# Both halves of a row of exponentials in a row on VectorE, and its sum scaled on ScalarE

## What is computed

```python
x = L0_attn_x                                    # (4, 2048, 256) fp32
x = x + _layernorm(_L0_attn_ref(_layernorm(x)))  # first stage
x = x + _layernorm(_L0_ffn_ref(_layernorm(x), ...))

def _L0_attn_ref(x):
    scores = jnp.einsum('bid,bjd->bij', x, x)
    attn = jax.nn.softmax(scores, axis=1)
    context = jnp.einsum('bij,bjd->bid', attn, x)
    return context
```

## Time and profile before

| | |
|---|---|
| median of 3 runs | 3178.43 us (3177.80 to 3181.57) |
| profiled execution, span | 3177.2 us |
| PE busy | 2982.5 us (94%) |
| DVE busy | 2656.8 us (84%) |
| ACT busy | 1847.9 us (58%) |
| POOL busy | 1754.4 us (55%) |
| TensorE's mean granted clock | 0.976 of full speed |
| first stage, until its last store is issued | 707.65 us |
| exponential stage of each of four batches | 70.2 us |

### The profile page before, as it was taken

One profiled execution on the slowest core, in us unless ns is written; L12 is line 12 of the kernel. 1 busy time (PEld: TensorE's weight loads), 2 busy tenths in 40 slices (PEclk: granted clock), 3 DMA queues, 4 the chain that ended last, 5 costly groups with the idle time before them and its releaser, 6 DMA issues.

```text
span 3177.2 us, 79721 instructions
## 1 busy us (share of the span) xinstructions
PE 2982.5 (94%) x24952; PEld 2581.8 (81%) x24952; DVE 2656.8 (84%) x7754; ACT 1847.9 (58%) x4226; POOL 1754.4 (55%) x2083
## 2 busy tenths in 40 slices
PE   6898989783899999999999999999999999999997
PEld 3676767573688888888888888888888888888886
DVE  6878788755788888888888888899998999999895
ACT  4233241402566666666666666666676676676673
POOL 1231314024566666666666666676676676676773
PEclk9999999995899999999999999999999999999999
DMA  1120202025111111111111111222112212122221
GB/s 38 38 70 28 80 14 87 4 83 205 33 50 49 53 51 49 52 48 49 54 50 50 50 48 50 56 56 60 56 55 57 65 55 60 55 55 60 63 56 46
DMA packets 273326, 177.65 MB, mean 56 GB/s; under 512 B 95758, under 2 KB 271090, under 8 KB 272754
## 3 DMA queue, kind: packets, MB, share of 16 engines
q1 hardware_dynamic: 273138, 175.50, 19.0%
HBM read 104.08 MB, written 54.54 MB: 50 GB/s over the span
## 4 chain that ended last, share of the span: by engine, by line
PE 72%; POOL 1%; issue 1%; DVE 0%; DMA 0%; ACT 0%; POOLq 0%; SPq 0%; DVEq 0%; ACTq 0%
PE b_ps L824 17%; PE b_ps L899 14%; PE b_ps L910 10%; PE b_ps L852 8%; PE b_ps L840 7%; PE b_ps L878 6%; PE b_ps L865 6%; PE b_ps L809 2%; PE b_ps L802 2%; PE b_ps L791 1%; POOL b_sq L1145 0%; POOL b_rn L1178 0%; POOL b_t L1167 0%; POOL b_kr L1183 0%; DVE b_probs L1093 0%
## 5 line engine op out<-in xcount | busy, mean ns | idle before, releaser
L957 ACT ACTIVATE b_probs<-b_probs,b_negmax 128x256 f32<-128x256 f32 x1024 | 506.0, 496 | 78.3 <-DVE b_negmax L1093 77.5
L824 PE MATMUL b_ps<-b_wqkv,b_hT_hi 128*128 128x512 f32 x1536 | 493.0, 402 | 1.0 <-DVE b_hT_lo L981 1.0
L899 PE MATMUL b_ps<-b_h2T,b_w 128*128 128x256 f16 x4224 | 473.0, 273 | 6.5 <-DMA b_h2T<-b_xh_hl 6.4
L899 PEld LDWEIGHTS b_ps<-b_h2T,b_w 128*128 128x128 f16 x4224 | 413.6, 98 | 55.1 <-DMA b_h2T<-b_xh_hl 6.8
L1145 POOL TENSOR_TENSOR b_sq<-b_sq 128x512 f32<-128x512 f32 (+5 forms) x768 | 419.3, 546 | 62.4 <-ACT b_sq L938 22.3
L1178 POOL TENSOR_TENSOR b_rn<-b_ss_min,b_mhalf 128x16 f32<-128x16 f32 x128 | 377.2, 2947 | 108.9 <-DVE b_ss_min L1005 108.7
L1106 DVE TENSOR_SCALAR b_probs<-b_probs,b_rinv 128x256 f32<-128x256 f32 x1024 | 409.6, 442 | 18.2
L1155 POOL TENSOR_TENSOR b_rstd<-b_var,b_mhalf 128x1 f32<-128x1 f32 x128 | 72.2, 564 | 552.3 <-DVE b_var L1066 552.3
L407 PE MATMUL a_ps<-a_xn_hl,a_E 128*128 128x256 f16 x3072 | 352.5, 277 | 18.9 <-DVE a_E L290 18.9
L407 PEld LDWEIGHTS a_ps<-a_xn_hl,a_E 128*128 128x128 f16 x3072 | 303.3, 99 | 58.5 <-issue 19.9
L910 PE MATMUL b_ps<-b_w,b_hid 128*128 128x256 f32 x1536 | 342.2, 379 | 1.2 <-DVE b_hid L1129 1.2
(11 more groups left out here) (137 smaller groups left out, 6191.6 us busy)
## 6 DMA issues: line engine op xcount, KB each, us to landing
b_hx<-xs_dram SPq DMA_DIRECT2D x256, 64.0 KB, 1.9
b_rot<-rot_dram SPq DMA_DIRECT2D x128, 128.0 KB, 2.1
b_xr<-xs_dram SPq DMA_DIRECT2D x128, 128.0 KB, 2.1
xp_dram<-b_xp SPq DMA_DIRECT2D x128, 128.0 KB, 1.7
b_h<-xp_dram SPq DMA_DIRECT2D x256, 64.0 KB, 1.8
a_x_res<-in_L_attn_x_dram SPq DMA_DIRECT2D x64, 128.0 KB, 2.2
x_dram<-a_x SPq DMA_DIRECT2D x64, 128.0 KB, 1.7
xs_dram<-a_xo SPq DMA_DIRECT2D x64, 128.0 KB, 1.8
```

The costliest lines, as they stand in the source:

```text
L824: last = nc.tensor.matmul(ps[:, bank, :], hT[:, k, :], wqkv[:, ds(layer(s), 1), part, k, bank * INNER:(bank + 1) * INNER], start=(k == 0 a ...
L899: last = nc.tensor.matmul(ps[:, bank, half * 2 * P:(half + 1) * 2 * P], w1[:, ds(layer(2 * j), 1), wp, k, first:first + P], h2T[:, hp, k, ...
L957: nc.scalar.activation(probs[:, h, :], probs[:, h, :], ACT.Exp, bias=negmax[:, h:h + 1], scale=-1.0, accum_out=rowsum[:, h:h + 1]).then_in ...
```

## The change

`row_sum` goes away. The scaling of the sum becomes an ACTIVATE on ScalarE, a copy with a scale, right behind the exponential whose sum it takes, after a wait for that very exponential. On VectorE each row now has reciprocal, high half, low half, one directly behind the other, and then the next row.

```diff
@@ -272,11 +272,6 @@
-            def row_sum(g):
-                u = g % 2
-                dve.wait_ge(e_full, g + 1)
-                nc.vector.tensor_scalar(colsum_s[:, u:u + 1], colsum[:, u:u + 1], 1.0 / XS_SCALE, None, ALU.mult).then_inc(sum_scaled, 1)
-
             def high_part(g):
                 u = g % 2
                 dve.wait_ge(sum_scaled, g + 1)
@@ -325,13 +320,9 @@
             for b in range(B):
                 first = b * WPB
-                row_sum(first)
-                high_part(first)
-                for g in range(first + 1, first + WPB):
-                    row_sum(g)
-                    low_part(g - 1)
+                for g in range(first, first + WPB):
                     high_part(g)
-                low_part(first + WPB - 1)
+                    low_part(g)
                 next_stats(first + WPB)
                 next_norm(first + WPB)
                 for g in range(first, first + WPB):
@@ -357,6 +348,8 @@
                     wait(act, e_lo, g - 1)
                     nc.scalar.activation(e32[:, u, :], scores, ACT.Exp, bias=negn[:, b % 2, j:j + 1], accum_out=colsum[:, u:u + 1]).then_inc(e_full, 1)
+                    act.wait_ge(e_full, g + 1)
+                    nc.scalar.activation(colsum_s[:, u:u + 1], colsum[:, u:u + 1], ACT.Copy, scale=1.0 / XS_SCALE).then_inc(sum_scaled, 1)
```

## The result

| | median | range | against the kernel before, same chip |
|---|---|---|---|
| kernel before | 3178.79 us | 3177.80 to 3181.57 | |
| changed kernel | 3155.34 us | 3154.23 to 3157.28 | 0.9926 (0.9912 to 0.9940) |

The change makes the kernel 23.5 us faster. Forecast was 3139.0, 39.5 us less than before, and 3155.3 lies above the range of 3128 to 3150. The span of the profiled execution went from 3177.2 to 3153.7 us.

A forecast was written before the change was run, and what follows sets the result against it. The exponential stages were taken as bound by a ring of waits between VectorE and ScalarE. Profiled span 3177.2 less 39.5 gives 3137.7, plus 1.3 for the median: 3139.0 us, range 3128 to 3150.

The forecast's parts named there:

- The ring of waits and its opening: Exponential stages: exponential and low half alternate at 4.54 us a row; the new order gives 3.78, saving 39.5 us in four.
- the sum 1.38 us early: Late rows of exponentials: the scaled sum is ready 1.4 us before VectorE's turn, covering ScalarE's added work.
- the price of the scaling on VectorE: Exponential stages: keeping the scaling on VectorE in the new order costs 0.19 us a row, 6 us in all.
- rival B: First context products: the ring opens and TensorE's clock also stays high, giving 3129.7 us or in between; chance 0.20.
- the sum kept 9.3: First context products: half-speed clock loses some 9.3 us over four batches; the forecast kept this loss as today.
- C: Exponential beside low half: the two engines disturb each other, 7 to 14 us longer, 3146 to 3153; chance 0.10.
- D: Exponential stages: the scaling makes ScalarE reload its function table and become the bound, +55 us, 3234; chance 0.03.
- E: Exponential stages: a wait still ties each exponential to the previous row; only 3 us gained, 3176; chance 0.03.
- No instruction of them moves: Later stages: their instructions stay put, so the first stage's gain, 39.5 us, moves all that follows.

The follow-up runs named there:

- Experiment 4: Kernel before with only VectorE's order changed (both halves of a row together), the sum's scaling left on VectorE: 3148.15 us, ratio 0.9899.
- experiment 1: Changed kernel plus 64 one-column memsets on VectorE at the start of the second stage's setup, restoring its instruction count: 3138.0 us, ratio 0.9864.

## Why the prediction was wrong

- **The ring of waits and its opening: right.** Turn 3.78 us, stage 60.39 (about 60.3 forecast), 39.3 us in four stages against 39.5, the sum 1.38 us early against 1.4, waits for it 42.3 against some 45. The new instruction is 0.20 us, the value taken. Experiment 4 shows the price of the scaling on VectorE at 5.8 us against 6.
- **The clock (rival B): partly.** The first 96 products take, in batch 0 and batch 1 after the change:

```profile
99.87 12.31 PE L400 MATMUL a_ps<-a_xn_hl,a_E 128*128 128x256 f16 x96 [3.41 <-DVE a_E L285]
...
258.89 10.64 PE L400 MATMUL a_ps<-a_xn_hl,a_E 128*128 128x256 f16 x96 [3.41 <-DVE a_E L285]
```

  Behind the same gap of 3.41 us one batch starts at a falling clock, the other at the full one (against 13.13 and 13.40 in the earlier trace rows, and 12.75 and 12.90 in the other two batches before). Batch 2 is like batch 1, batch 3 like batch 0, so 3.3 us are lost at these products where the sum kept 9.3. Which batches are hit differs between executions: in experiment 1, whose first stage is the same program, they are 0, 2 and 3. In return the first scores of batches 1 to 3 run into half speed, which the prediction hadn't looked at. In balance the second stage starts 43.2 - 39.3 = 3.9 us earlier than the exponential stages account for, which is put down to the clock; it is not 9.3 and not 0.
- **C and D: out.** The low half is 2.35 us beside an exponential, and no table load stands among the new instructions. **E** is out with the turn of 3.78.
- **The step that failed** is "No instruction of them moves", from which it followed that a gain in the first stage moves all that follows. The start of the second stage did move, by 43.2 us; the stage itself became 19.7 us longer. No instruction of it was reordered, but all of VectorE's were shifted by 64, and 17.9 of the 19.7 are the 13 passes of the first layer's loop. The effect was in no term and in no rival, and nothing in the trace of before pointed to it by time; what was there to read was that one of two nearly equal loops is fetched in every pass and the other not. What the runs showed in its place: the start of that loop's code decides whether VectorE waits for a second transfer of code behind the loop's head, 1.4 us a pass, 18 us in 13.
- With the placement put right (experiment 1) the kernel takes 3138.0, 1 us from the forecast. That is partly luck: the 3.9 us of the clock were won, and the second stage is 3.5 us longer than before (3137.3 - 666.6 against 2467.2), of which 2.3 lie before the first `kT_low` and 1.2 between the first and the fifth (75.9 us before, 77.0 here, 72.7 to 77.0 in all these kernels). In both stretches TensorE's granted clock stands at 0.50 for part of the time, at other moments in each kernel; whether that is all of it, and of the 4.4 us in experiment 4, was not settled.

## What to carry to other kernels

Where an engine's instruction count changes ahead of a loop, compare the transfers of the instruction queues before and after, in the stretch of each loop and not in total, and look for "issue" idle time at the loop's head, above all a second one behind the first: a stage whose code is the same can still change its time. A few empty instructions ahead of the loop settle whether that is it, and may be the whole cure. Where two buffers bring nothing, look for the queue in which the instruction that frees one stands behind an instruction that needs the other.

## What the runs showed of the hardware

- VectorE's program came in transfers of 8192 bytes, five in each pass of a loop of 321 or 349 instructions at some placements and none at others. At the head of a loop the next started 2.4 us after the one before, and the engine went on 1.2 to 1.6 us after the landing of the one it waited for. A wait for the first of them left the pass at 73.1 us, a second wait made it 74.5. A shift by 12 to 64 instructions of unchanged code moved the time by 16 to 18 us in 3150.
- A wait of ScalarE for its own exponential costs next to nothing: the scaling starts 0.03 us behind the accumulator's read (94.28 against 94.06 + 0.19), and is 0.20 us long.
- The exponential and the low half do not disturb each other: 1.97 and 2.34 us in the kernel before, where they never overlap, 1.97 and 2.35 us together.
- The same idle gap of TensorE, 3.41 us, was followed by a full clock in one batch and by 1.7 us of loss in another (12.31 against 10.64 for the same products).
